# Attention block: the ninth score tile's probabilities go onto the running total by an adding DMA, and one half's denominators move to the next group's third step

## What is computed

```
scores = jnp.clip(jnp.einsum('bhqd,bhkd->bhqk', Q, K), -80.0, 80.0)
scores = jnp.where(causal, scores, -jnp.inf)
weights = jax.nn.softmax(scores / jnp.sqrt(jnp.float32(d_qk)), axis=-1)
attn = jnp.einsum('bhqk,bhkd->bhqd', weights, V)
```

## Time and profile before

| | us |
|---|---|
| median of 3 runs | 3002.51 (3002.14 to 3005.1) |
| the profiled execution, its own time | 3003.13 |
| its span, first to last instruction | 3001.4 |
| TensorE busy | 2925.5 (97% of the span) |
| VectorE busy | 2684.1 (89%) |
| ScalarE busy | 1589.5 (53%) |
| GpSimd busy | 580.7 (19%) |
| mean granted TensorE clock | 0.993 of 2.4 GHz |

### The profile page before, as it was taken

How to read it: one execution, slowest core, us unless ns; L and a number is a source line. 1 busy time by engine, 2 the same in 40 slices (tenths; PEclk the granted TensorE clock), 3 DMA queues, 4 the chain that set the end, 5 groups by cost and what they waited for, 6 DMA issues and landing times.

```text
span 3001.4 us, 65378 instructions
## 1 busy us (share of the span) xinstructions
PE 2925.5 (97%) x22500; PEld 2134.2 (71%) x22500; DVE 2684.1 (89%) x4593; ACT 1589.5 (53%) x2330; POOL 580.7 (19%) x620
## 2 busy tenths in 40 slices
PE   7999899999999999969999999999999999999999
PEld 6777644444444444458888888888888888888887
DVE  7999788888888888869999999999999999999996
ACT  5666578778778778643333333333333333333333
POOL 3444300000000000012222222222222222222221
PEclk9999999999999999989999999999999999999999
DMA  7889956566566566441222222222222221221220
GB/s 241 283 288 301 285 126 148 131 147 143 133 150 137 137 151 135 130 127 54 58 60 60 60 60 59 51 58 58 59 60 60 59 59 54 56 58 57 59 57 30
DMA packets 335143, 333.27 MB, mean 111 GB/s; under 512 B 60368, under 2 KB 242512, under 8 KB 335056
## 3 DMA queue, kind: packets, MB, share of 16 engines
q1 hardware_dynamic: 335056, 332.26, 40.7%
HBM read 215.52 MB, written 116.65 MB: 111 GB/s over the span
## 4 chain that ended last, share of the span: by engine, by line
PE 56%; DVE 1%; ACT 0%; DMA 0%; POOL 0%; issue 0%; SPq 0%; DVEq 0%
PE p_ring L2010 21%; PE p_ring L2036 16%; PE ps_od L2010 12%; PE ps_od L1990 6%; PE p_ring L2024 1%; PE ps_od L2036 0%; PE p_ring L2052 0%; PE p_ring L2017 0%; DVE sb_wg_lo L1908 0%; PE p_ring L1990 0%; DMA sb_x<-in_L_attn_x_dram 0%; DVE sb_wd_lo L1908 0%; DMA dn<-sb_x_big 0%; DVE sb_x_amax L106 0%; DVE sb_x_big L118 0%
## 5 line engine op out<-in xcount | busy, mean ns | idle before, releaser
L1063 ACT ACTIVATE sb_probs<-scores 128x1024 f32<-128x1024 f32 (+3 forms) x512 | 405.8, 840 | 112.8 <-PE scores L1269 106.5
L1657 POOL TENSOR_TENSOR sb_stage<-sb_stage,sb_h_inv 128x512 f32<-128x512 f32 (+1 forms) x192 | 190.4, 992 | 866.6 <-DVE sb_h_inv L112 866.6
L2010 PE MATMUL p_ring<-sb_wg_hi,sb_xq_hi 128*128 128x512 f32 (+1 forms) x1024 | 294.8, 369 | 0.3 <-DVE sb_wd_lo L1908 0.3
L2010 PE MATMUL p_ring<-sb_wg_lo,sb_xq_hi 128*128 128x512 f32 (+1 forms) x1024 | 290.6, 365 | 0.0
L2010 PE MATMUL p_ring<-sb_wg_hi,sb_xq_lo 128*128 128x512 f32 (+1 forms) x1024 | 289.4, 363 | 0.0
L2036 PE MATMUL p_ring<-sb_wd_hi,sb_ht_hi 128*128 128x512 f32 x693 | 278.8, 402 | 0.0
L2036 PE MATMUL p_ring<-sb_wd_hi,sb_ht_lo 128*128 128x512 f32 x693 | 274.2, 396 | 0.0
L2036 PE MATMUL p_ring<-sb_wd_lo,sb_ht_hi 128*128 128x512 f32 x693 | 273.7, 395 | 0.0
L1269 PEld LDWEIGHTS scores<-sb_q_hi,sb_k_hi 32*128 32x128 f32 x1536 | 73.6, 182 | 280.7 <-ACT sb_probs L1063 156.6
L811 POOL TENSOR_TENSOR sb_at_in<-sb_at_in,sb_inv_in 128x512 f32<-128x512 f32 x64 | 95.0, 1484 | 910.4 <-DMA sb_inv_in<-dinv 910.1
L1727 ACT ACTIVATE sb_stage<-sb_stage,sb_code_zero 128x512 uint8<-128x512 f32 (+1 forms) x192 | 139.5, 727 | 241.8 <-DVE sb_stage L122 241.8
(11 more groups left out here) (215 smaller groups left out, 7202.4 us busy)
## 6 DMA issues: line engine op xcount, KB each, us to landing
kq<-sb_kq_out SPq DMA_DIRECT2D x32, 1024.0 KB, 7.2
sb_kq_raw<-kq SPq DMA_DIRECT2D x64, 512.0 KB, 6.9
sb_xin<-in_L_attn_x_dram SPq DMA_DIRECT2D x32, 512.0 KB, 6.9
v<-sb_v_out SPq DMA_DIRECT2D x64, 256.0 KB, 6.5
rq<-sb_r_out SPq DMA_DIRECT2D x64, 256.0 KB, 4.5
sb_qr<-rq SPq DMA_DIRECT2D x32, 512.0 KB
sb_kr_hi<-kr SPq DMA_DIRECT2D x32, 512.0 KB
sb_kr_lo<-kr SPq DMA_DIRECT2D x32, 512.0 KB
```

Of the source, the lines that this page charges most:

```text
L1063: act.activation(probs(k)[:, 2 * pair:2 * pair + 2, off:BANK], scores[(2 * k + pair) % RING2][:, :, off:BANK], ACT.Exp, scale=SCALE).then_ ...
L1657: pool.tensor_tensor(x, x, spread(h_inv[:, a // QB:b // QB], (b - a) // QB), ALU.mult).then_inc(h_y, 1)
L2010: i = pe.matmul(ps[:, m, 0:b0 - a0], xt[a][:, c, :], wg[b][:, m, c, a0:b0], start=(c == 0 and a == b == 0), stop=(c == DC - 1 and a == 1))
```

## The change

Step 8 is no longer a denominator operand of its own. GpSimd waits until the total of steps 4 to 7 stands and step 8 is clipped, runs a 128x1 tensor_tensor, and issues a DMA that reads step 8's probabilities (128x2048 float32, 1024 KB) and adds them to `added[:, 0]` in SBUF. TensorE's TOTAL waits for this DMA (`fifth_added`) instead of for `total`; ScalarE waits for it before step 2 of the next group overwrites the buffer of step 8.

The second half's denominators (TOTAL, 9, 10, 11) all move to index 2 of the next group. Those of the first half are done at indices 4 (step 0), 5 (step 1) and 6 (steps 2 and 3). ScalarE's copies move to index 2 of the next group (before: 0) and to index 7 (before: 6).

```
-DENOMS = [0, 1, 2, 3, 8, 9, 10, 11, TOTAL]
-DENOMS_AT = {3: [0], 4: [1], 5: [2], 6: [3], 9: [8], 11: [9]}
-DENOMS_NEXT = [10, 11, TOTAL]
+DENOMS = [0, 1, 2, 3, TOTAL, 9, 10, 11]
+DENOMS_AT = {4: [0], 5: [1], 6: [2, 3]}
+NEXT_STEP = 2
+FIFTH = 8
+DENOMS_NEXT = [TOTAL, 9, 10, 11]
 DENOMS_HALF = 4
-DENOM_STEP = 6
+DENOM_STEP = 7
...
         @block.gpsimd
         def _(pool):
-            ahead.divide_tile(pool, 0, 16 * NI, 16)
+            pool.memset(passed[:], 0.0).then_inc(sums_seen, 1)
+            pool.wait_ge(sums_seen, 1)
+
+            def body(it2, s, first, last):
+                if last:
+                    ahead.divide_tile(pool, 0, 16 * NI, 16)
+                pool.wait_ge(clipped, step_no(it2, s, FIFTH) + 1)
+                pool.wait_ge(total, totals(it2, s) + 2)
+                own(pool, sums_seen, it2 * 2 + (s + 1))
+                pool.tensor_tensor(passed[:], passed[:], passed[:], ALU.add).then_inc(sums_seen, 1)
+                pool.dma_start(added[:, 0], probs(FIFTH), accum_op=ALU.add).then_inc(fifth_added, 16)
+
+            groups(pool, body)
...
+                if k - PROBS + NS == FIFTH and not first:
+                    before = preceding(it2, s)
+                    act.wait_ge(fifth_added, before[0] * 32 + (before[1] * 16 + 16))
...
-                    if k == 0 and not first:
+                    if k == NEXT_STEP and not first:
                         copy_denominators(*preceding(it2, s), 1)
...
                 if k == TOTAL:
-                    pe.wait_ge(total, totals(it2, s) + 2)
+                    pe.wait_ge(fifth_added, it2 * 32 + (s * 16 + 16))
...
+                    if k == NEXT_STEP and not first:
                         for x in DENOMS_NEXT:
                             denominators(*preceding(it2, s), x)
```

More of the change, by code:

```diff
@@ L879, in attention @@
         total = sem("total")
+        fifth_added = sem("fifth_added")
+        sums_seen = sem("sums_seen")
+        passed = sb("passed", [P, 1])
         at_stored = [sem(f"at_stored{h}") for h in range(HALF)]
```

## The result

| | predicted | measured |
|---|---|---|
| changed kernel, us | 3322 (3150 to 3500) | **3395.86** median of 4 (3389.17 to 3399.14) |
| kernel before, us | | 3003.81 median of 4 (3002.14 to 3005.31) |
| ratio | 1.106 | 1.1303, 95% interval 1.1283 to 1.1322 |
| attention's period for two groups | near 77 | 77.4 to 84.4, 81.2 in the mean (before 56.6) |
| mean granted clock | under 1.00 in attention | 0.941 over the run (before 0.993) |

Slower, as forecast, and by 392 us instead of 319. Three rows of the page of the changed kernel: the adding transfers' queue, the queue that brings instructions (36 packets before, 152 now), and GpSimd's 128x1 instruction, whose mean is far above the 0.19 us of the earlier trace rows.

The account below looks back on a forecast made before the run. ScalarE's loop and VectorE's stretch at a group's end were taken to bound the kernel. Stall 5.8, index 2 2.2, first half 0.4 and clock 1.7 gave 10.1 us at 31 boundaries, 313, plus 7: 3322 us (3150 to 3500).

Parts of the forecast that it names:

- places of the denominators: Four denominators behind step 3's score at index 2 cost 2.2 us a group, those of the first half 0.4.
- clock behind the pause: TensorE pauses some 5.9 us in every group, then runs at half speed for 3.4 us, losing 1.7 us.
- the stall by the transfer itself: ScalarE's exponential of step 2 waits for the DMA: 8.5 less 2.7 us of slack, 5.8 us a group.
- the floor of 2.58 us: In attention, the loop with ScalarE lets no full step of TensorE be shorter than 2.58 us.
- I give it nothing: The removed 0.88 us denominator and other room freed on TensorE bring no time; they become more waiting.
- The new wait: From the total through GpSimd and the DMA until ScalarE may overwrite step 8's buffer in step 2: 8.5 us.
- the second read: The adding DMA must also read its destination, 1.05 MB at 403 GB/s: 2.6 us more.
- 0.3 for GpSimd: GpSimd's share of the wait ahead of the DMA: 0.19 us for its instruction, the rest guessed for a semaphore.
- the first half's denominators: Moved to indices 4 to 6: index 3 gains 0.2 us, index 5 loses 0.2, index 6 0.4; together +0.4.
- the skill's transfer rule: GpSimd's DMAs take 2.0 us plus bytes over 436 GB/s: 4.4 us here, stall 2.0, about 3148 us in all.
- a DMA that starts late: Rival: the DMA starts only when VectorE's stretch ends, 6.4 us past the total; 3528 us, chance 0.10.
- SyncE, "nothing": The d store and four loads behind it go out some 2 us later on SyncE, at no cost.

Follow-up runs that it names:

- after_48: The changed kernel with 48 warm-up matmuls instead of 32: 3400.87 us (ratio 1.1317).
- places_only_48: The changed kernel without the adding DMA, step 8 left out of the sums, denominators where the change puts them, 48 warm-up matmuls: 3079.28 us (1.0248).
- fillers_24: no_gpsimd_op_48 with 24 more matmuls before the score of step 3, and 28 warm-up matmuls: 3294.1 us (1.0963).
- no_gpsimd_op_48: The changed kernel with 48 warm-up matmuls and a semaphore increment in place of GpSimd's 128x1 instruction: 3348.92 us (1.1143).
- before_without_8: The kernel before without step 8's denominators, which its sums then lack, and the total in two pieces: 2993.21 us (0.9958).
- early_add: The changed kernel with the DMA started once step 8 is clipped, onto the first sum, final additions behind it, denominators moved, 40 warm-up matmuls: 3119.49 us (1.0382).

## Why the prediction held, and what it mis-sized

By the experiments the loss of after_48, 396 us, is 12.8 us at each of 31 boundaries; the changed kernel itself lost 392.

| term, us a group | predicted | measured | by |
|---|---|---|---|
| places of the denominators | 2.6 (2.2 + 0.4) | 2.4 | places_only_48 |
| clock behind the pause | 1.7 | 1.8 (2.3 by the rows) | fillers_24 |
| GpSimd's instruction held | 0 (a rival) | 1.7 | no_gpsimd_op_48 |
| the stall by the transfer itself | 5.8, and 0.2 for the end | 6.9, the end included | what remains |
| sum | 10.3 | 12.8 | after_48 |

- **What bounds the kernel.** Right in that the loop with ScalarE and VectorE's stretch decide, not TensorE's busy time. But the row from which the floor of 2.58 us was read shows none: 1.37 + 0.46 + 0.65 + 0.10 is 2.58, so TensorE's work fills it. The floor is there all the same: from the score of step 5 to that of step 6 the kernel before takes 2.55 us for some 2.35 of work at the prediction's prices.
- **Removed denominators, "I give it nothing".** Wrong for the kernel as it was: 0.4 a group could be had (before_without_8). In the changed kernel the room went to the wait, as forecast.
- **The new wait.** The mechanism, the place and the releaser are as forecast: ScalarE at step 2, one transfer a group. The transfer's 5.6 us for a plain 1 MB and 2.6 for the second read became 5.1 and 2.7. The 8.5 us from total to exponential are what no_gpsimd_op_48 shows, 8.53 and 8.66, though it has no instruction of GpSimd in them. Behind this agreement lies the error: "0.3 for GpSimd" counted the instruction at the earlier trace rows, 0.19 us, and a guess. It takes 0.50 us or 3.17. That is **the step that failed**, 1.7 of the 2.5 us missing.
- **The other 0.8.** The split by differences puts it on the stall, but the rows of no_gpsimd_op_48 do not. From the total to the score of step 3 they have 9.2 us where the kernel before has 3.6: 5.7 more, for a stall forecast at 5.8. The excess lies behind that score: 30.0 us to the next total where there were 24.7, 5.3 more, for a forecast of 4.3 (2.2 + 0.4 + 1.7). The four denominators took 2.2 (3.65 against 1.49), the clock 2.3, and what is left, the first half's denominators above all, 0.8 for 0.4: index 3, from the score of step 4 to that of step 5, was forecast to get 0.2 shorter and got 0.2 longer (3.25 or 2.71 us against 2.79).
- **Places, 2.6 against 2.4.** This agreement is in part luck. In places_only_48 the stretch behind the score of step 3 is 3.1 us longer, and the one ahead of it 0.7 shorter, 2.9 us from the total to the score where it was 3.6: TensorE has lost the denominators of index 0. With the transfer in place that 0.7 goes into the wait, and about 3.0 remain: fillers_24 has 27.7 us from the score of step 3 to the next total, the kernel before 24.7. So in the table "places" is too small by some 0.6, and "what remains" too large by that and by the clock's 0.5.
- **The trace and the skill's transfer rule.** The plain copy of 1 MB landed 5.1 us after its issue, the adding one 7.8. The fit of the Trainium skill (DMA: Bandwidth & Descriptors, Anatomy of one DMA) gives, as an estimate, 4.4 us for these bytes: near the copy and far from the adding transfer, for which it would have to count the destination's read as well (6.8). Taking the trace's own load was the better choice.
- **The rival "a DMA that starts late".** Half right. VectorE's stretch does hold GpSimd in one kind of group, but what is held for long is the small instruction, and only until 3.3 us behind the total, since in these groups the stretch ends there and not at the 6.4 us read from the earlier trace rows. The rule of the Trainium skill that the prediction cited (SBUF — State Buffer, SBUF: two separate sides) speaks of the writing of descriptors. The trace agrees with it at most for a single clip: the DMA instructions of no_gpsimd_op_48, 0.94 and 1.52 us, end about 0.1 us behind a clip's end. The same section has the port that the two engines share taken for a whole instruction. That fits the hold in kind but not in length: one 128x1 instruction was held across five of VectorE's instructions, four ends among them.
- **Clock.** Right in kind, and short by 0.6 us: 2.3 by the rows, against 1.7 worked out from a pause elsewhere in the trace of before. Such a row can be carried over for a first size. The run fillers_24 agrees with 1.7 better than it should, by the delay that the fillers cause.
- **SyncE, "nothing".** Right here by luck of the longer period. In early_add, with a period of 32 us, the loads behind a delayed store cost TensorE 65 us of waiting.
- **Not foreseen at all:** the pause for instructions. It costs nothing in the changed kernel (after_48) and would have cost 87 us in a faster one.

## What to carry to other kernels

A transfer that somebody waits for costs its whole landing less the slack of the buffer that it holds: look for the next writer of its source, not only for the reader of its result, start it as soon as its operands stand, and follow what the moved waits hold up in every queue, SyncE's too. An instruction that is there only to pass a wait on should not be one that reads and writes SBUF: here a 128x1 one was held for 3.17 us beside VectorE, and a semaphore increment did the same for 1.7 us a group less. And whenever an edit changes the number of instructions ahead of or in a long loop, compare the packets of the instruction queue before believing the time: 16 small matmuls more or fewer moved an unchanged loop by 100 us.

## What the runs showed of the hardware that was not expected

- **TensorE's loop and its instructions.** The loop has some 1640 recorded instructions in the kernel before (824 matmuls and 816 weight loads in two groups, 788.47 to 845.05 us). With 36 packets on the instruction queue it returns to its start without a pause; shifted by 16 matmuls it pauses at each return, at 152 packets: 116 packets more, for 13 returns. With 28 fillers a group and a longer loop it was 135. The Trainium skill (Runtime: NRT & Kernel Launch, Instruction fetch mechanics) gives TensorE's instruction memory 2048 instructions in blocks of 256, and has a taken branch fetch its target if that isn't in a window of two pages. The 2048 fit a loop that lies in few enough blocks or in one too many, according to where it starts. The window of two pages does not fit: by it every return of this loop would fetch, and the kernel before shows no wait there and no packet more. The exact limit was not measured, and that these waits are such fetches rests on the packets and on their place at each return.
- **An adding transfer within SBUF** costs one more read of its bytes: 7.8 us for 1 MB against 5.1 for the copy, and 5.2 for an addition of 512 KB.
- **GpSimd beside a busy VectorE.** The 128x1 tensor_tensor, 0.19 us alone, took 3.10 to 3.20 us in all 16 groups of the first kind in after_48, each time to within 0.1 us of the end of VectorE's stretch. In the second kind it took 0.50 to 0.54 us in 15 groups and 3.45 in one, although VectorE's rows have no gap there either.
- **Two ways to lose the same time.** With the pause for instructions the transfer let ScalarE go 10.8 us behind the total also in the short kind of group (840.85 against 830.05), not 8.65 as without it, yet the whole time is the same. It is the landing itself that is later, 10.0 us from the issue instead of 7.9. The granted clock is 0.50 and back sooner in that kernel, whose pause had begun sooner:

```profile
841.00:845.00 4.00, 3.50 (x36) 1.84 (x40) 1.12 (x3) 1.87 (x3) 0.00 (x0) 0.50 0.00 1
845.00:849.00 4.00, 3.88 (x60) 1.75 (x52) 0.97 (x2) 2.56 (x5) 0.00 (x0) 0.98 0.02 4
```

In after_48 it is 0.57 still in the 4 us from 856, where the exponential had come at 852.65. Why the landing is later, and why the two balance so closely, was not tested.
